# Message-passing and expert layers on one core: empty places of the sorted lists read a row by partition instead of row 0

## What is computed

```python
x = x + _L0_gnn_ref(_layernorm(x), edge_index, W, a_l, a_r)        # attention: softmax over edges with the same src
x = x + _L0_ffn_ref(_layernorm(x)[None], ..., w1, b1, w2, b2)[0]   # feed-forward on the 1561 best-weighted nodes
x = x + _L1_gnn_ref(_layernorm(x), src, dst, edge_type_4, ...)     # mean over edges with the same dst of x[src] @ rel_W[type]
x = x + _L1_ffn_ref(_layernorm(x)[None], router_w, w1, b1, w2, b2)[0]  # 8 experts, each node goes to its best 2
```

## Time and profile before

| | |
|---|---|
| median of 3 runs | 1973.9 us (1972.54 to 1975.08) |
| the profiled execution | 1972.32 us, span 1970.6 us |
| GpSimd (POOL) busy | 1373.6 us, 70% |
| TensorE matmul (PE) busy | 1431.9 us, 73% |
| VectorE (DVE) busy | 1305.9 us, 66% |
| ScalarE (ACT) busy | 575.1 us, 29% |
| gathers of the attention | 464, issued from 231.9 to 819.8 us |
| gathers of the relation layer | 440, issued from 1134.7 to 1685.1 us |

### The profile page before, as it was taken

The page is one execution under the profiler, slowest core; times in us unless marked ns, Lnnn a source line. Parts: engine busy times, 40 slices in busy tenths (PEclk is TensorE's granted clock), DMA queues, the critical chain, the costliest instruction groups (busy, mean ns, idle before and its releaser), DMA issues.

```text
span 1970.6 us, 22614 instructions
## 1 busy us (share of the span) xinstructions
PE 1431.9 (73%) x6252; PEld 937.2 (48%) x6252; DVE 1305.9 (66%) x2938; ACT 575.1 (29%) x1687; POOL 1373.6 (70%) x1383
## 2 busy tenths in 40 slices
PE   5666477788888887579999966677676777457970
PEld 3333256655655555457784433334333333246860
DVE  6999878798888887485993044544444444666544
ACT  0687411156666662132333300000000000342320
POOL 0788577777777777778877277777777777546771
PEclk9799788889999999789999989988767667557995
DMA  5111143445544444602004563333333333312337
GB/s 93 12 31 28 33 106 104 108 118 132 136 117 115 129 106 106 74 1 63 2 1 116 150 206 104 106 106 104 105 106 105 104 105 103 48 47 78 101 104 214
DMA packets 105416, 183.74 MB, mean 93 GB/s; under 512 B 31178, under 2 KB 69533, under 8 KB 105170
## 3 DMA queue, kind: packets, MB, share of 16 engines
q0 software_dynamic: 56384, 134.58, 27.6%
q1 hardware_dynamic: 47603, 45.16, 8.5%
q10 hardware_dynamic: 1308, 2.56, 0.5%
HBM read 151.56 MB, written 30.38 MB: 92 GB/s over the span
## 4 chain that ended last, share of the span: by engine, by line
POOL 34%; PE 25%; DVE 19%; issue 13%; DMA 7%; ACT 1%; DVEq 1%; SPq 0%; POOLq 0%; ACTq 0%
POOL gath L898 32%; DVE hot_c L641 6%; PE ps L932 6%; PE ps L1321 4%; DMA gath<-y_tab,index_b 4%; PE ps L1283 4%; PE ps L1269 3%; DVE hot_r L632 2%; PE ps L1710 2%; PE ps L1721 2%; DMA wide<-y_nodes 1%; DMA gath<-h_tab,index_a 1%; DVE acc L923 1%; POOL y_nodes L1682 1%; DVE gath L971 1%
## 5 line engine op out<-in xcount | busy, mean ns | idle before, releaser
L932 PE MATMUL ps<-gath,hot 128*125 128x260 f32 (+1 forms) x1808 | 615.6, 476 | 296.0 <-DVE gath L971 108.0
L932 PEld LDWEIGHTS ps<-gath,hot 128*125 128x125 f32 x1808 | 354.1, 221 | 517.3 <-DMA gath<-y_tab,index_b 196.8
L898 POOL DMA_INDIRECT gath<-h_tab,index_a x464 | 447.6, 965 | 150.0 <-issue 138.4
L898 POOL DMA_INDIRECT gath<-y_tab,index_b x440 | 417.4, 949 | 166.8 <-issue 123.2
L923 DVE TENSOR_TENSOR acc<-acc,ps 125x257 f32 (+1 forms) x672 | 284.0, 423 | 328.4 <-PE ps L932 299.1
L673 PE MATMUL ps<-hot_c,pay 125*128 125x440 f16 (+1 forms) x901 | 194.4, 369 | 63.9 <-ACT pay L662 59.7
L728 POOL DMA_INDIRECT slot_tab_b<-sent_word_b,sent_to_b x136 | 165.0, 1213 | 36.3 <-issue 36.3
L718 POOL DMA_INDIRECT slot_tab<-sent_word,sent_to x102 | 130.4, 1279 | 82.3 <-DVE sent_to L480 51.5
L662 ACT ACTIVATE pay<-hot_r,plan_b 125x128 f16<-125x128 f16 x578 | 172.0, 386 | 0.0
L673 PEld LDWEIGHTS ps<-hot_c,pay 125*128 125x128 f16 x901 | 87.7, 101 | 162.3 <-ACT pay L662 81.2
L971 DVE TENSOR_TENSOR gath<-gath,ps 128x1024 f32<-128x1024 f32 x116 | 135.9, 1212 | 0.0
(11 more groups left out here) (330 smaller groups left out, 2026.6 us busy)
## 6 DMA issues: line engine op xcount, KB each, us to landing
y_tab<-ybuf SPq DMA_DIRECT2D x25, 448.0 KB
gath<-h_tab,index_a POOLq DMA_INDIRECT x464, 2.8
gath<-y_tab,index_b POOLq DMA_INDIRECT x440, 2.8
h_tab<-hbuf SPq DMA_DIRECT2D x25, 113.8 KB
xa<-in_x SPq DMA_DIRECT2D x1, 2800.0 KB
xa<-in_x SPq DMA_DIRECT2D x5, 560.0 KB
xn_tab<-acc SPq DMA_DIRECT2D x25, 112.0 KB
out<-xa SPq DMA_DIRECT2D x5, 560.0 KB
```

Source lines behind the costliest of these rows:

```text
L898: p.indirect_dma_start(gath[:, ring(k) + s, 0:width], None, table, bass.IndirectOffsetOnAxis(ap=index[g][:, col:col + 1], axis=0)).then_in ...
L932: ins = t.matmul(ps[0:NP, 4 + q % 2, 0:width], hot[:, s, :], gath[:, s, 0:width], start=(e == 0), stop=(e == n - 1))
```

## The change

Three lists are touched. A row number that depends on the partition, 23 times the partition (0 to 2921, inside every table), is made once by an iota of one column, `away`.

- In both sorts, `spread_tail` adds that number to the index of each empty place (`local` below 0) in the columns from 408 on (`TAIL` = 51 is the group, 408 the column): 56 columns in sort a, 32 in sort b. It is two VectorE instructions, the second waiting for the first; for a it runs at group 3 of the attention, for b at group 25 of the relation layer. GpSimd waits for the matching count of `tail_spread` ahead of the gathers of group 51.
- In the experts' list the empty places (`node_f` 0) get 23 times the partition instead of 0. That is one more VectorE instruction (`away_e`), and the one that makes `node_i` moves behind the next wait.

The one-hots, the sums and `dest_i` are made from the same numbers as before.

```diff
+TAIL = E // 128 // GRP
+AWAY = 23
...
+    away = base.tile("away", [128, 1])
...
+        p.iota(away[:, :], [[1, 1]], base=0, channel_multiplier=AWAY, allow_small_or_imprecise_dtypes=True)
         p.memset(ones_b[:, :], 1.0)
...
     def gather_group(p, k, table, width, g):
         per = GRP * 128 // unit[g]
+        if k == TAIL:
+            p.wait_ge(tail_spread, words[g])
...
+    def spread_tail(v, g):
+        at = slice(GRP * TAIL, cols[g])
+        rows = {"a": hi_s.bitcast(I32), "b": high_b}[g][:, 0:cols[g] - GRP * TAIL]
+        v.tensor_scalar(rows, local[g][:, at], 0.0, away[:, 0:1], ALU.is_lt, ALU.mult).then_inc(vector_step, vn.up())
+        v.wait_ge(vector_step, vn.n)
+        v.tensor_tensor(index[g][:, at], index[g][:, at], rows, ALU.add).then_inc(tail_spread, 1)
...
             plan_b_read(v, k, 1)
+            if k == DEEP:
+                spread_tail(v, "a")
...
                 v.tensor_tensor(flat(xb, k), ps[0:NP, 1, 0:D], sb_s[:, :], ALU.add).then_inc(self_added, 1)
+            if k == NT:
+                spread_tail(v, "b")
...
         v.wait_ge(vector_step, vn.n)
+        v.tensor_scalar(away_e[:, :], node_f[:, :], 0.0, away[:, 0:1], ALU.is_equal, ALU.mult)
         v.tensor_scalar(empty[:, :], node_f[:, :], 0.0, None, ALU.is_equal)
-        v.tensor_scalar(node_i[:, :], node_f[:, :], -1.0, 0.0, ALU.add, ALU.max)
         v.scalar_tensor_tensor(dest_f[:, :], node_f[:, :], 2.0, kth[:, :], ALU.mult, ALU.add).then_inc(vector_step, vn.up())
         v.wait_ge(vector_step, vn.n)
+        v.scalar_tensor_tensor(node_i[:, :], node_f[:, :], -1.0, away_e[:, :], ALU.add, ALU.max)
         v.tensor_tensor(empty[:, :], empty[:, :], dump[:, :], ALU.mult).then_inc(vector_step, vn.up())
```

More of the change, by code:

```diff
@@ L83 @@
 assert GROUPS * GRP == COLS and COLS_B <= COLS and SORT_STEPS * SORT_N == EC and PSTEPS * CHAINS == EC
-assert MOE_TURNS * MOE_BODY == MOE_TILES and B_END + 8 <= GROUPS
+assert 127 * AWAY < N and MOE_TURNS * MOE_BODY == MOE_TILES and B_END + 8 <= GROUPS
 assert RANK_PHASE + (PSTEPS + 1) // 2 < B_PHASE
@@ L248, in build @@
     tile_id, row_id = end.tile("tile_id", [NP, 2, NT]), end.tile("row_id", [NP, 1])
-    node_f, kth, empty, dump, dest_f = (end.tile(n, [128, MOE_TILES]) for n in ("node_f", "kth", "empty", "dump", "dest_f"))
+    node_f, kth, empty, dump, dest_f, away_e = (
+        end.tile(n, [128, MOE_TILES]) for n in ("node_f", "kth", "empty", "dump", "dest_f", "away_e"))
     dest_i, node_i = (end.tile(n, [128, MOE_TILES], I32) for n in ("dest_i", "node_i"))
@@ L277, in build @@
     ends_turned, reach_ready, reach_summed = sem("ends_turned"), sem("reach_ready"), sem("reach_summed")
-    planned, slots_ready = sem("sorts_planned"), sem("slots_ready")
+    planned, slots_ready, tail_spread = sem("sorts_planned"), sem("slots_ready"), sem("tail_spread")
     var_ready, root_done, norm_ready = sem("var_ready"), sem("root_done"), sem("norm_ready")
```

## The result

The changed kernel takes 1967.39 us (median of 7 runs, 1966.34 to 1969.35) against 1972.93 us (7 runs, 1971.43 to 1975.08) of the kernel before, measured beside it: a ratio of 0.9972, 95% interval 0.9960 to 0.9984. That is 5.5 us, where the forecast was 13.7. The interval leaves out 1, so it is faster, but it lies outside the forecast's range (1957.0 to 1967.0 us), by 0.4 us. The profiled execution spans 1966.2 us (before 1970.6). Lines have moved: L906 gathers (L898 before), L734 sends (L728), L938 adds a group's sums (L923), L970 is the score step (L955), L1105 the large adds on GpSimd (L1088), L1129 the divisions (L1112), L1133 the statistics (L1116), L947 the sums on TensorE (L932).

The account below looks back on a forecast made before the run. GpSimd's gathers in the two graph layers, and their late landing at each layer's end, were taken as the bound. Terms 7.5 + 6.3 + 0 - 0.1 = 13.7 us gave 1973.9 - 13.7 = 1960.2 us, range 1957.0 to 1967.0.

Parts of the forecast that it names:

- Cause of the tail: Last gathers of both graph layers: empty places all reading row 0 slow the transfers, 0.37 us of backlog per gather.
- End of the relation layer: Last relation gather lands 2.8 us after issue instead of 9.07: 6.3 us gained, ends 5.5 and 6.8.
- End of the attention: Score step 8.4 us earlier, large adds on GpSimd starting 6.8 us earlier: 7.5 us gained, ends 6.0 and 8.4.
- sat idle for 6.81 us until VectorE's divisions let it begin L1088: Attention's end: GpSimd's idle time before its large adds read as a wait for VectorE, so 6.8 us could go.
- 0.5 us for slower sends: Attention's end: GpSimd's sends running beside VectorE's long instructions take longer, 0.5 us off the gain.
- The gain passes on whole: Behind the attention: statistics start the feed-forward layer's long VectorE chain, so the 7.5 us reach the end undiminished.
- Experts and the added instructions: Experts' last scatters gain 0 (up to 0.5 us); the added routing instruction costs 0.12 us, the other additions nothing.
- Slower: Rival, tail gathers: strided rows fall together worse than one row; at 1.9 us each 9 us slower, 1983 us; chance 0.05.
- row not the cause: Rival, both tails: the one row is not the cause or the index misses the gathers; 1974 us, chance 0.08.
- TensorE's clock: Rival, relation tail and routing: TensorE at 2.4 GHz instead of 1.2 saves 6.8 us more, 1953 us; chance 0.05.
- Half a cure: Rival, both tails: the empty columns' new rows leave half the backlog; 7.2 us gained, 1966.7 us; chance 0.10.
- an attention end that moved by 8 us with a feed-forward start that moved by much less than 7: Sign that the forecast is wrong, between attention and feed-forward layer; listed without a chance.

Follow-up runs that it names:

- run 9: The change with all empty places of the tail and the experts' list reading the one row 23: 1971.9 us beside 1971.4 of the kernel before, one execution each.
- run 14: The change kept for sort a alone, undone for sort b and the experts' list: 1973.14 us against 1970.8 of the kernel before, ratio 1.0012.
- run 15: The kernel before with the four large adds on VectorE instead of GpSimd: 1969.3 us, ratio 0.9992 to the kernel before.
- run 16: The kernel before with a one-column GpSimd add right behind the partition_all_reduce: 1970.06 us, ratio 0.9998 to the kernel before.
- run 10: The change kept for sort b alone, undone for sort a and the experts' list: 1964.74 us, ratio 0.9967 to the kernel before.
- run 11: The whole change plus a one-column GpSimd add right behind the partition_all_reduce: 1959.48 us, ratio 0.9938 to the kernel before.
- run 12: The whole change with the four large adds on VectorE instead of GpSimd: 1955.75 us, ratio 0.9922 to the kernel before.
- run 13: The whole change with ScalarE's square root moved ahead of the last feed-forward copy instead of the last three: 1964.68 us, ratio 0.9968 to the kernel before.
- run 17: The whole change with the large adds on VectorE and ScalarE's square root moved later: 1955.61 us, ratio 0.9925 to the kernel before.
- run 18: The whole change with neighbouring rows, distance 1 instead of 23, for the empty places: 1966.78 us, ratio 0.9977 to the kernel before.

## Why the prediction was wrong, step by step

**Cause of the tail: right**, and now shown (run 9). The part of the backlog that the 18 and 14 empty columns did not explain goes with it, so that too was of the empty places, whether in the partly empty columns or by a price above the 1.62 us taken.

**End of the relation layer: right**, 6.3 us forecast. The last gather lands 2.78 us after its issue, and from the last issue to the last add it takes 3.66 us instead of 10.47: 6.8 us less, the 6.3 of the landing and 0.5 of the last products. They take 0.70 us on TensorE against 1.24, at a granted clock of 1.00 (1689 to 1690 us) against 0.50, which was the upper end of this term. The layer as a whole gained 8.3 us in the two profiled executions (560.81 to 552.54). The other 1.5 us lie between the first issue and the last (548.88 instead of 550.34 us), were not in the sum and are not of the tail. All gathers of the relation layer (ns min/median/max), in the change and, under it, in run 14, where sort b's tail still reads one row:

```profile
L906 POOL DMA_INDIRECT gath<-y_tab,index_b x440: 942/946/998, 1138.1 to 1686.9; - x147
...
L906 POOL DMA_INDIRECT gath<-y_tab,index_b x440: 942/946/998, 1136.1 to 1685.0; - x147
```

Before, the median was 949 ns, and so it is in runs 15 and 16, which are edits of the kernel before; in all edits of the changed kernel it is 945 or 946 ns. That is 3 ns for each gather, 1.3 us in 440 and 1.4 us in the attention's 464. What in the changed program makes them shorter stays open. So the tail's worth is read among the kernels of the changed program: 552.3 to 552.6 us where sort b is treated (the change and runs 10 to 13, 17 and 18), 558.8 and 559.2 where it is not (runs 9 and 14), 6.6 us.

**End of the attention: wrong**, 7.5 us forecast, none gained. The step that failed is the sentence that GpSimd "sat idle for 6.81 us until VectorE's divisions let it begin L1088". The row said "<-issue", that is, waiting for nothing the profile shows, and I read a wait for VectorE into it because the division came to an end at a fitting time. The rows in hand spoke against it: by the prediction's own 1.4 us a division, the first large one was done at 849.0 us, 2.6 us before L1088 began, and L1088's view shows the two configuration instructions at 844.9. Without the switch GpSimd would indeed have waited for that division (run 16: 4.37 us, adds from 848.40), so in before both ended nearly together by accident. Held against the true chain (sends, 23.75 us; switch, 6.81; adds, 12.79), the end of the attention's gathers was never on the path; all of that chain starts at the last issue. With the switch in its place the prediction's own terms give 1.3 us (adds of 11.5 us; they took 11.42) less 0.5 for slower sends, some 0.8 us instead of 7.5. Between the two profiled executions the chain went as follows: last issue 1.9 us earlier (817.90 and 819.79; 1.4 of it is the shorter gathers), sends 2.5 us longer, switch 0.9 longer, adds 1.4 shorter, together 0.1 us later. The Trainium skill (GPSIMD Engine Reference, Instruction dispatch) says that the first call of a freshly loaded kernel on GpSimd pays a load of about 6 us, with no instruction of its own in the profile. The trace agrees in kind: 6.7 to 7.7 us of nothing between the two configuration instructions and the add, and 5.6 to 6.2 us ahead of the all-reduce. It should have been one of the rivals.

**"0.5 us for slower sends": mis-sized.** They became 2.5 us slower (26.25 against 23.75), since VectorE's long work moved on top of them: no send behind the last gather takes over 1.8 us in the kernels with an untreated tail in sort a, and the longest take 2.5 us in those with a treated one. In kernels of the changed program the last statistics start 1.6 us later for it in the mean, which uses up what the shorter gathers had brought.

**"The gain passes on whole": not what cost it.** The 3.2 us lost between 864 us and the relation layer all lie between the gates' input w_col and the relation's first gather: 239.1 us in this execution of before, 242.3 in this one of the change. Runs 9 to 12, 14 to 16 and 18, with and without any part of the change, all lie between 239.8 and 241.0, so these two executions lie on either side of all those, and the stretch does not follow the change: I take the 3.2 us for the chance of two executions, not for a price of the change. What differs between draws can be seen in part: VectorE's 25 small comparisons (L1188, L1171 before) take 0.35 us each alone and up to 0.93 where they meet one of GpSimd's adds; together 10.8 us in before, the least of all, and 13.0 in the change, whose ranking also began 0.5 us later. That is not all of it, since runs 10 and 18 have 13.0 us as well and a stretch of 240.9 and 241.0; what else differs, and what sets that sum, stays open. ScalarE's root ahead of its copies hands such a delay on to TensorE; with it moved (run 13) the stretch takes 237.7 us. The parts do not close to better than 2 or 3 us: from the profiles of the changed program, 6.6 us at the end of the relation layer and some 3 us by shorter gathers in the two layers, less 1.6 at the end of the attention, would be about 8 us, where 5.5 were measured (3.2 to 7.9 by the interval); runs 10 and 14 together, 6.7 and -2.3, would be 4.4.

**Experts and the added instructions: right.** From the start of the last node_f (L1652, L1633 before) to that of dest_i it is 1.14 us (1777.92 to 1779.06) instead of 0.94: 0.20 us for the added instruction, where 0.12 were taken. Behind the last add of the relation layer all kernels take 274.8 to 276.6 us, with or without them. The last scatter is issued 9.8 us after the last tile's result was added (1923.51 and 1913.69), 8.7 us before.

**The rivals.** "Slower" and "row not the cause" are excluded by the landings, and TensorE's clock stayed at its lower level in the routing (granted 0.50 at 1710 to 1745 us, as in the earlier trace rows). "Half a cure" named 1966.7 us, next to the 1967.39 measured, but for another reason: no half of a backlog was left. That the number is close is luck. The case that was missing is the one the last lines of the prediction name as a sign, "an attention end that moved by 8 us with a feed-forward start that moved by much less than 7", without a mechanism and a chance of its own.

## What to carry to other kernels

When an indirect gather has empty places, give each of them a row of its own; neighbouring rows were enough here. Read "idle, <-issue" literally: an engine that stands for several us there, for nothing shown, may be busy with something of its own. Ask for the rows of the line behind it, its sequencer's too, before you put the idle time down to a neighbour. A change that brings the neighbour's work forward then gains nothing until that time is moved; here a one-column operation, put where the engine had to wait anyway, both showed it and removed it. A gain at the end of a stage has to be followed on every engine that starts its own chain at the last issue, not only on the one that was seen to wait.

## What the runs showed of the hardware

- Gathers whose 128 places all read one row of 1 KB keep the DMA engines 83 to 90% busy at 75 to 80 GB/s, where different rows, scattered or next to each other, need 35 to 39% for 104 to 107 GB/s. Rows 0 and 23 do it alike.
- GpSimd needs 6.7 to 7.7 us between a partition_all_reduce and the next ordinary tensor operation, wherever that comes, even with 464 gathers and 16 sends in between (where it waits for nothing else); gathers and sends don't need it. The profile shows a pair of MODIFY_POOL_CONFIG of its sequencer at the start of that time, at 844.9 us before and at 223.2 in run 11. The all-reduce itself stands behind 5.6 to 6.2 us of the same kind, with such a pair at their start (216.5 us in the change).
- In every profiled execution of the changed program and its edits a gather of the relation layer occupies GpSimd for 945 or 946 ns at the median, in those of the kernel before and its edits for 949, on the same chip too (runs 14 and 15). No run shows why.
- A send on GpSimd takes 1.18 us alone and up to 2.51 beside VectorE's large multiplications in the change; an add of 125x1280 takes 2.87 us on GpSimd there, up to 4.14 beside such a multiplication in before, and 1.42 on VectorE (run 12).
- On two of the chips the kernel takes 2230 us, and there neither this change nor any of the edits above can be told from nothing.
